# Softmax reciprocals as a power on GpSimd, with all five instruction orders laid out anew, in a one-core decoder layer

## The reference, cut to what matters

```
x = x + attention(layernorm(x))                  # 16 heads, 16-wide keys, 64-wide values
x = x + cross_attention(ctx, ctx, layernorm(x))  # features exp(z), exp(-z); 64 context rows
x = x + ffn(layernorm(x))                        # token mix, sigmoid gate, squared relu

# attention: the softmax runs over the QUERIES (axis 1 of b n h m)
sim  = einsum('bnkh,bmhk->bnhm', q, k)
attn = softmax(sim / 4, axis=1)
o    = einsum('bnhm,bmhv->bnhv', attn, v)

# cross attention
scores = einsum('nqhd,nkhd->nhqk', qf, kf) / 16
attn   = softmax(scores, axis=-1)
out    = einsum('nhql,nlhd->nqhd', attn, vf) @ fc_w.T + fc_b
```

## Time and profile before

| what | value |
|---|---|
| median of 3 runs | 479.99 us (479.38 to 481.4) |
| profiled execution | 479.61 us, of which 477.8 us are the span of the core |
| TensorE busy | 93% of the span |
| VectorE, ScalarE, GpSimd busy | 79%, 63%, 28% |
| mean granted TensorE clock | 0.982 of full speed |
| data moved by DMA | 34.02 MB |

### The profile page before, as it was taken

The page is one execution under the profiler, slowest core; times in us unless marked ns, Lnnn a source line. Parts: engine busy times, 40 slices in busy tenths (PEclk is TensorE's granted clock), DMA queues, the critical chain, the costliest instruction groups (busy, mean ns, idle before and its releaser), DMA issues.

```text
span 477.8 us, 7930 instructions
## 1 busy us (share of the span) xinstructions
PE 445.1 (93%) x2588; PEld 276.3 (58%) x2588; DVE 379.9 (79%) x689; ACT 299.0 (63%) x732; POOL 134.5 (28%) x181
## 2 busy tenths in 40 slices
PE   7779979999999999999999999999999999896985
PEld 3553426535655676557565675566556664485774
DVE  6567676786999988886999989777999787669664
ACT  4348866577688756565796856655796668323431
POOL 2511113113623351214431442114332413142410
PEclk9979999999999999999999999999999999897999
DMA  7852210133221001323301301333102000000001
GB/s 257 309 173 108 78 68 18 45 110 123 101 86 59 12 1 34 114 68 119 105 26 47 105 6 45 113 116 118 59 16 77 36 2 0 23 0 23 2 1 44
DMA packets 20013, 34.02 MB, mean 71 GB/s; under 512 B 2308, under 2 KB 6660, under 8 KB 19844
## 3 DMA queue, kind: packets, MB, share of 16 engines
q1 hardware_dynamic: 19972, 33.52, 21.5%
HBM read 23.02 MB, written 10.49 MB: 70 GB/s over the span
## 4 chain that ended last, share of the span: by engine, by line
PE 75%; DVE 9%; issue 5%; ACT 5%; DMA 3%; POOL 1%; SPq 0%; ACTq 0%; DVEq 0%; POOLq 0%
PE av_bank L653 18%; PE m_bank L591 9%; PE m_bank L593 7%; PE m_bank L592 7%; PE s_pair L639 7%; ACT e_sb L862 4%; DVE nmax L1060 3%; PE m_bank L782 3%; PE m_bank L831 3%; DMA q_parts<-qkt_lo 3%; PE m_bank L795 3%; PE m_bank L770 2%; PE m_bank L820 2%; PE av_bank L603 2%; PE m_bank L670 2%
## 5 line engine op out<-in xcount | busy, mean ns | idle before, releaser
L862 ACT ACTIVATE e_sb<-s_pair,nmax 128x512 f32<-128x512 f32 x256 | 172.8, 690 | 55.9 <-DVE nmax L1060 55.9
L1060 DVE TENSOR_REDUCE nmax<-s_pair 128x2 f32<-128x1024 f32 x128 | 152.9, 1214 | 20.2 <-PE s_pair L639 19.3
L653 PE MATMUL av_bank<-e_sb,v_sb 128*64 128x512 f32 x512 | 124.5, 607 | 4.5 <-POOL v_sb L1330 2.4
L1330 POOL TENSOR_TENSOR v_sb<-v_sb,rsum 128x256 f32<-128x256 f32 x64 | 39.6, 619 | 179.3 <-DVE rsum L1068 169.5
L653 PEld LDWEIGHTS av_bank<-e_sb,v_sb 128*64 128x64 f32 x512 | 31.6, 136 | 57.8 <-issue 46.6
L639 PE MATMUL s_pair<-q_st,k_st 64*128 64x512 f32 x256 | 50.6, 457 | 9.5 <-issue 6.8
L862 ACT ACTIVATION_READ_ACCUMULATOR e_sb<-s_pair,nmax 128x1 f32 x256 | 53.4, 208 | 0.0
L639 PEld LDWEIGHTS s_pair<-q_st,k_st 64*128 64x128 f32 x256 | 21.2, 186 | 55.3 <-issue 35.0
L1357 POOL TENSOR_TENSOR sx<-sx,xrec 128x512 f32<-128x512 f32 x24 | 24.8, 1043 | 46.4 <-DVE xrec L1240 46.4
L591 PE MATMUL m_bank<-wo_hi,ot_hi 128*128 128x256 f32 x120 | 34.9, 291 | 0.0
L593 PE MATMUL m_bank<-wo_lo,ot_hi 128*128 128x256 f32 x120 | 33.5, 279 | 0.0
(11 more groups left out here) (179 smaller groups left out, 857.9 us busy)
## 6 DMA issues: line engine op xcount, KB each, us to landing
q_st<-q_parts SPq DMA_DIRECT2D x31, 256.0 KB, 7.7
k_st<-k_parts SPq DMA_DIRECT2D x62, 128.0 KB
q_parts<-qkt_hi SPq DMA_DIRECT2D x8, 256.0 KB
q_parts<-qkt_lo SPq DMA_DIRECT2D x8, 256.0 KB
out<-x_sb SPq DMA_DIRECT2D x8, 256.0 KB, 2.1
k_parts<-qkt_hi SPq DMA_DIRECT2D x7, 256.0 KB, 2.5
k_parts<-qkt_lo SPq DMA_DIRECT2D x7, 256.0 KB, 5.9
x_sb<-in_x SPq DMA_DIRECT2D x3, 512.0 KB, 9.1
```

The source lines that it names most:

```text
L653: mm = pe.matmul(av_bank[n % AV_BANKS][64 * par:64 * par + 64, :], v_sb[:, m, 2 * p + par, :], e_sb[:, (4 * q + 2 * i + par) % E_RING, :], ...
L862: act.activation(e_sb[:, g % E_RING, :], s_pair[k // 2][:, k % 2, :], ACT.Exp, bias=nmax[:, g % 8:g % 8 + 1], accum_out=esum[:, q % 4, k:k ...
L1060: dve.tensor_reduce(nmax[:, at:at + 2], s_pair[i][:, :, :], AX_X, ALU.max, negate=True)\
L1330: pool.tensor_tensor(v_sb[:, m:m + 2, 2 * p:2 * p + 2, :], v_sb[:, m:m + 2, 2 * p:2 * p + 2, :], rsum[:, q % 4, :].rearrange("p (m h) -> p ...
```

## The change

All reciprocals of softmax sums go from VectorE to GpSimd, as the sum to the power of -1. The power is a two-input instruction with a tile of constants, `minus_one`. On VectorE the unit `rsum` is gone, and the sum of `xn` tells GpSimd directly. ScalarE's `exp` gets one more wait, since `esum` is now read by GpSimd. Every table is laid out anew, `feat` among them. The reciprocal units first:

```diff
+        minus_one = sb("minus_one", [P, 8])
...
                 act.wait_ge(nmax_ready, 2 * q + k // 2 + 1)
+                if q >= 4 and k == 0:
+                    act.wait_ge(v_scaled, q - 3)
...
-            def row_sums(_, q):
-
-                dve.wait_ge(exp_ready, 4 * q + 4)
-                if q >= 4:
-                    dve.wait_ge(v_scaled, q - 3)
-                dve.reciprocal(rsum[:, q % 4, :], esum[:, q % 4, :]).then_inc(rsum_ready, 1)
-
...
                 dve.wait_ge(xexp_ready, n + 1)
-                link(dve.tensor_reduce(xsum[:, n % 4, :], x_tile(n).rearrange("p (h l) -> p h l", h=8),
-                                       AX_X, ALU.add))
                 if n >= 4:
                     dve.wait_ge(xp_ready, n - 3)
-                dve.reciprocal(xrec[:, n % 4, :], xsum[:, n % 4, :]).then_inc(xrec_ready, 1)
+                dve.tensor_reduce(xsum[:, n % 4, :], x_tile(n).rearrange("p (h l) -> p h l", h=8),
+                                  AX_X, ALU.add).then_inc(xsum_ready, 1)
...
+            pool.memset(minus_one[:, :], -1.0).then_inc(pool_chain, 1)
...
                 p, m = (q // 2) % NP, 2 * (q % 2)
-                pool.wait_ge(rsum_ready, q + 1)
+                pool.wait_ge(exp_ready, 4 * q + 4)
...
+                pool.tensor_tensor(rsum[:, q % 4, :], esum[:, q % 4, :], minus_one[:, 0:4], ALU.pow).then_inc(rsum_ready, 1)
+                pool.wait_ge(rsum_ready, q + 1)
...
                 n = 8 * b + 2 * t + gg
+                pool.wait_ge(xsum_ready, n + 1)
+                pool.tensor_tensor(xrec[:, n % 4, :], xsum[:, n % 4, :], minus_one[:, :], ALU.pow).then_inc(xrec_ready, 1)
                 pool.wait_ge(xrec_ready, n + 1)
```

Of the tables, the rows that the prediction speaks of (some 150 rows change; the signs are those of the whole tables):

```diff
-    ("ld", 0, (4,), dict(sp=61)),
+    ("ld", 0, (4,), dict(sp=103)),
...
-    ("ld", 0, (3,), dict(sp=31)),
+    ("ld", 0, (3,), dict(sp=100)),
...
-    ("ld", 0, (5,), dict(sp=89)),
+    ("ld", 0, (5,), dict(sp=190)),
...
-    ("ld", 0, (6,), dict(sp=137)),
+    ("ld", 0, (6,), dict(sp=190)),
...
-    ("ld", 0, (7,), dict(sp=178)),
+    ("ld", 0, (7,), dict(sp=217)),
...
-    ("qk", 1, (0, 0), dict(pe=206, act=207, dve=206, sp=230)),
+    ("qk", 1, (0, 0), dict(pe=215, act=208, dve=216, sp=209)),
...
-    ("qk", 1, (0, 1), dict(pe=223, act=221, dve=220, sp=235)),
+    ("qk", 1, (0, 1), dict(pe=222, act=226, dve=228, sp=218)),
...
-    ("ld", 1, (2,), dict(sp=284)),
+    ("ld", 1, (2,), dict(sp=315)),
...
-    ("ld", 1, (1,), dict(sp=249)),
-    ("ld", 1, (0,), dict(sp=235)),
+    ("ld", 1, (1,), dict(sp=283)),
+    ("ld", 1, (0,), dict(sp=224)),
...
-    ("load", ("x1",), dict(sp=-1)),
+    ("load", ("x1",), dict(sp=-941)),
...
-    ("feat", (), dict(dve=-190, act=-192)),
+    ("feat", (), dict(sp=31, dve=31, act=34)),
...
-ATTENTION = dict(scores=12, weigh=42, max=(11, 12), exp=(17, 17, 18, 18), rsum=27, scale=22, ot_hi=39, ot_lo=44)
+ATTENTION = dict(scores=12, weigh=43, max=(11, 12), exp=(17, 17, 19, 19), scale=-10, ot_hi=37, ot_lo=44)
```

More of the change, by code:

```diff
@@ L67 @@
[L67 to L77, removed]
@@ new lines @@
+    ("kv", (), dict(pe=-24, dve=-28)),
+    ("ln2", (0,), dict(dve=77, pool=84, do=84)),
+    ("t2", (0,), dict(pe=143, act=98, dve=92)),
+    ("op", (1, 1), dict(pe=82, dve=82)),
+    ("ln2", (1,), dict(dve=90, pool=87, do=126)),
+    ("z", (0, 0), dict(act=160)),
+    ("t2", (1,), dict(pe=489, act=243, dve=251)),
+    ("z", (0,), dict(pe=381)),
+    ("z", (0, 1), dict(act=170)),
+    ("xs", (0, 0), dict(dve=262, act=254)),
+    ("z", (1, 0), dict(act=259)),
+    ("xs", (0,), dict(pe=925)),
+    ("xs", (0, 1), dict(dve=270, act=272)),
@@ new lines @@
+    ("xn", (0, 0), dict(dve=300, pool=129)),
+    ("xs", (1,), dict(pe=1251)),
+    ("xs", (1, 1), dict(dve=501, act=504)),
+    ("xn", (1, 0), dict(dve=501, pool=161)),
+    ("xn", (0, 1), dict(dve=499, pool=129)),
+    ("z", (1,), dict(pe=1242)),
+    ("z", (1, 1), dict(act=270)),
+    ("xs", (1, 0), dict(dve=311, act=308)),
+    ("xn", (1, 1), dict(dve=796, pool=161)),
+    ("xs", (2, 0), dict(dve=683, act=684)),
+    ("pt", (0, 0), dict(pe=1788, act=553)),
+    ("pt", (0, 1), dict(pe=1790, act=624)),
@@ new lines @@
+    ("xs", (2,), dict(pe=1615)),
+    ("xs", (2, 1), dict(dve=864, act=866)),
+    ("xn", (2, 0), dict(dve=992, pool=976)),
+    ("xs", (3,), dict(pe=1647)),
+    ("xs", (3, 1), dict(dve=1186, act=1773)),
+    ("pt", (1, 1), dict(pe=1810, act=1108)),
+    ("xn", (2, 1), dict(dve=1125, pool=1169)),
+    ("xs", (3, 0), dict(dve=1121, act=1113)),
+    ("pt", (1, 0), dict(pe=1792, act=693)),
+    ("pv", (0, 0), dict(pe=1811, act=1109, dve=1186)),
+    ("pt", (2, 0), dict(pe=1877, act=1194)),
+    ("pv", (0, 1), dict(pe=1811, act=1193, dve=1186)),
@@ L222 @@
-    ("load", ("x1",), dict(sp=-1)),
-    ("load", ("fc",), dict(sp=-355)),
-    ("load", ("rest",), dict(sp=-2172)),
-    ("load", ("feat",), dict(sp=-822)),
-    ("v", (0, 0), dict(pe=27, act=24)),
-    ("v", (0, 1), dict(pe=14, dve=23)),
-    ("v", (0, 2), dict(pe=-5, act=-24)),
-    ("v", (0, 3), dict(pe=15, dve=31)),
+    ("warm", (0, 2), dict(pe=-401)),
+    ("warm", (1, 2), dict(pe=-1504)),
+    ("warm", (2, 2), dict(pe=-1616)),
+    ("ln1", (0,), dict(dve=-1829, pool=-1804, do=-1644)),
+    ("ln1", (1,), dict(dve=-1646, pool=-1634, do=-1644)),
@@ new lines @@
+    ("cut", ("first",), dict(act=-785, dve=-877)),
+    ("cut", ("qk",), dict(act=-1402, dve=-1483)),
+    ("t1", (0,), dict(dve=-1487, pe=-1479, act=-1485)),
+    ("t1", (1,), dict(pe=-414, act=-891, dve=-1483)),
+    ("first", (0,), dict(pe=-104, act=-69, dve=-62)),
+    ("first", (1,), dict(pe=-44, act=-9, dve=-10)),
+    ("qk", (0, 0), dict(dve=-393, sp=-386, pe=-114, act=-451)),
+    ("qk", (0, 1), dict(pe=-97, act=-96, dve=-149, sp=-333)),
+    ("cut", ("v0",), dict(act=-487, dve=-488)),
@@ L230 @@
+    ("cut", ("v1",), dict(act=-143, pool=-132)),
+    ("ld", (1,), dict(sp=-32)),
+    ("load", ("o",), dict(sp=-2017)),
+    ("ld", (2,), dict(sp=41)),
+    ("load", ("x1",), dict(sp=-941)),
+    ("load", ("fc",), dict(sp=-88)),
+    ("load", ("rest",), dict(sp=-956)),
+    ("load", ("feat",), dict(sp=-442)),
+    ("v", (0, 0), dict(pe=14, act=20)),
+    ("v", (0, 1), dict(pe=23, dve=24)),
+    ("v", (0, 2), dict(pe=-9, act=-9)),
+    ("v", (0, 3), dict(pe=27, dve=42)),
 ]
 ONCE = [
-    ("cut", ("o",), dict(act=-195, pool=-202)),
@@ L269, in orders @@
         out["act"] += [(at + a["exp"][k], "exp", 0, (q, k)) for k in range(4)]
-        out["dve"].append((at + a["rsum"], "rsum", 0, (q,)))
         out["pool"].append((at + a["scale"], "scale", 0, (q,)))
@@ L1293, in _ @@
                      "ln1_do": apply_on_vector(1), "ln2_do": apply_on_vector(2), "ln3_do": apply_on_vector(3), "t1": t1,
-                     "t2": t2, "pv": pv, "max": maxima, "rsum": row_sums, "ot_lo": ot_low,
+                     "t2": t2, "pv": pv, "max": maxima, "ot_lo": ot_low,
                      "qk": qk, "v": v, "op": op, "feat": feat, "kv": kv, "xs": xs, "xn": xn_, "fc": fc,
```

286 lines of the change are left out of this document (122 added, 164 removed).

## The result

The changed kernel takes 521.06 us (median of 4 runs, 519.78 to 521.4) beside 480.06 for the kernel before (4 runs, 479.38 to 481.4): a ratio of 1.0845, 95% interval 1.0816 to 1.0875. It is 8.5% slower. The forecast of 498 us had the direction and the first cause, and was 23 us short; 521 lies outside its range. The span went from 477.8 to 519.2 us.

A forecast was written before the change was run, and what follows sets the result against it. The prediction took TensorE, busy for 445.1 of 477.8 us, to bound the kernel. Late loads, stalls, power and last batch, less the start's gain, summed to +18.5 on 479.6 us: 498 us, range 480 to 511.

The forecast's parts named there:

- The late loads: Loads that SyncE issues behind stores arrive late and TensorE waits; with the clock loss after stalls, 20.1 us.
- three long stalls: Scores of quads 14, 30 and 46 wait for loads queued behind query stores: +12.2 us, bounds 5.3 and 14.
- three short ones: Scores of quads 20, 36 and 52 wait for loads behind key stores: +3.6 us, bounds 2 and 13.
- pair 8: Its load queues on SyncE behind the late load of pair 7: +0.7 us, bounds 0 and 2.
- behind the stalls: After each long stall TensorE loses clock and waits a little again: 1.2 us each, +3.6, bounds 0 and 6.
- the last batch: Earlier sums against slower power on GpSimd and no gap-filling `warm` products: +0.5 us, bounds -2.6 and +8.
- The power: Reciprocals as power on GpSimd delay `weigh`: +1.5 us in quads 1 to 8, +0.7 in 60 to 63, hidden in the middle.
- GpSimd has room: Claim that GpSimd can take 86 us of powers on top of its 134.5 us of work.
- the power goes by element: Rival, chance 0.2: 128 x 8 takes 2.2 us on GpSimd, lengthening the last batch and `weigh`: 507 us.
- The start: Feature-map table moved behind quad 1's maxima; quad 2's scores come at 33.4 us: -4.3 us, bounds -5.8 and -1.
- TensorE's busy time about unchanged: Sign expected in the changed kernel's trace: TensorE's total busy time stays about as before.

The follow-up runs named there:

- a_sp: The changed kernel with SyncE's order of stores and loads as in the kernel before, all else kept: 498.11 us, ratio 1.0358 to the kernel before.
- a_sp_xrec: The changed kernel with SyncE's order as before and only cross attention's reciprocal back on VectorE, the quads' sums still a power on GpSimd: 479.4 us, ratio 0.9969.
- a_sp_rec: The changed kernel with SyncE's order as before and all reciprocals back on VectorE: 479.16 us, ratio 0.9965 to the kernel before.
- a_rec: The changed kernel with all reciprocals back on VectorE, its other orders and late loads kept: 501.69 us, ratio 1.0445 to the kernel before.
- b_k16: The kernel before with a load's key DMAs as four of 32 rows instead of two of 64: 481.0 us, ratio 0.9994.
- b_sp: The kernel before with only SyncE's order of stores and loads taken from the changed kernel: 506.51 us, ratio 1.0532.

## Why the prediction was right and wrong

**The late loads (right).** Forecast +12.2 for three long stalls, +3.6 for three short ones, +0.7 for pair 8 and +3.6 behind the stalls, 20.1 together. Taking them away gives 22.5 to 22.95. Read off the lags of the change against a_sp: 15.2 at the three long ones (5.1, 4.8, 5.35), 7.3 at the short ones and 7.6 in the quad behind the long ones, less 4.3 at quads 16 and 32, whose own load was late anyway. The rest, -3.1, is spread, 1.7 of it in the last batch. The 12.3 us from store to use were right to 0.3 in four places. The short ones were sized too small: from the key store to quad 20's scores it took 10.8 us (126.78 to 137.60), where the 1.2 taken came to 9.8. That is less than the 12.3 behind query stores, as the prediction had it. The term of +3.6 after a stall counted 1 us of clock for each, 3 in all. The clock stayed at half for six us behind quads 14 and 30 and for about four behind quad 46, and TensorE's busy time is 5.7 us longer than in a_sp.

**The power (the step that failed).** "In the middle, TensorE has 1 us and more of other work ahead of `weigh`, which hides that" weighed only the power ahead of a quad's scaling. By a_sp_xrec that one is indeed free. The powers of cross attention stand in the same queue ahead of it, and those were costed at nothing in the middle. By the lags of a_sp less those of a_sp_rec, the power costs 0.2 us up to quad 8 (forecast +1.5), 10.9 from there to quad 59 (forecast 0), 0.2 to quad 63 (+0.7), and 7.7 in the last batch (+0.5). The spans differ by 18.9 where the terms sum to 2.7. "GpSimd has room: 64 x 0.8 + 32 x 1.1 = 86 us on top of 134.5" is the flaw in one line. It is true of the span and false of the 15 us in which four tiles and two scalings fall together. The price was also short, 1.1 us taken against 1.64, though within the bounds 0.7 and 2.2. The rival "the power goes by element" (507 us, 0.2) has +7.5 in the last batch, close to these 7.7, but from a price of 2.2 that was too high, and the middle was missing there as well.

**The start (right in place, not in worth).** -4.1 us at quad 8, forecast -4.3; first scores at 20.31, quad 2's at 33.08 (forecast 21 and 33.4). Most of it is given back by quad 23 even with SyncE's order as before; the forecast took the remaining new orders as neutral.

**Where the missing 23 us are.** The sum had +18.5, and the span grew by 41.4. Of the 22.9 between them, 16.2 are the power (18.9 for 2.7), 2.6 the late loads (519.2 less 496.5 is 22.7, for 20.1), and 4.1 the rest of the change (a_sp_rec's span is 0.2 under the kernel before's, for the -4.3 of the start). No bound covered the largest part: the power in the middle had neither a term nor an upper bound. Nor did the upper end of 511 take in the sum of the upper bounds that were given, which is 527.6. The last batch as a whole lost 3.6 us, inside its bounds, because the new orders gain 1.5 us there without the power (a_rec) and the power costs 5.1 us on top. "TensorE's busy time about unchanged" was wrong too, by 8.8 us.

The GPSIMD Engine Reference of the Trainium skill, section Key points, has elementwise work about twice as fast on VectorE. The measured pairs are a reciprocal on VectorE against a power on GpSimd, 170 against 1010 ns and 203 against 1638: the direction agrees, and the factor is six to eight.

## What to carry to other kernels

Weigh work that moves to an idle engine against the stretch in which that engine's queue is fullest, and not against its share of the span: list its instructions of that stretch, add the new ones, and compare with the stretch's length. Where a queue also holds units that others need soon, the price is set by what stands ahead of them. A load moved behind a store in an in-order queue inherits the store's wait and its traffic; if a load has no slack, first make the transfer itself short, then its place matters less (27.6 us here for a different split of the same bytes).

## What the runs showed of the hardware

The same 256 KB of keys, queued behind two stores of queries, take 10.4 us from their first issue to the scores as two DMAs whose outer dimension is 2 (98.48 less 88.05), and 6.7 as four of 32 rows (96.84 less 90.17). The four take longer to issue, 2.70 us for 1.27. DMA: Bandwidth & Descriptors in the Trainium skill, section Why a DMA increments its semaphore by 16 and not by 1, has the slowest dimension cap the engines used; the trace agrees: at a DMA share of 0.13 the two took some five us to move, and at 0.61 and more the four were through in two or three (b_k16). The runs changed the number of DMAs and the dimension together. After stalls of 4.71 and 5.01 us TensorE ran for six more at the 1.2 GHz level (granted clock 0.50), and in b_sp the stalls made 5.6 us of busy time without any added product. By the three measured forms (703, 1010 and 1638 ns) a power on GpSimd costs about 0.39 us and 0.155 us for each element of a partition.
